# A 12-stage decoder on one core: head maxima subtracted by broadcast weights, a rebuilt last attention stage, new tables, loads and order

## The reference

```
log_D[t, s] = cs[t] - cs[s] + igate[s]    (s <= t)
D = exp(log_D - max_s log_D);   C = (q k^T / 4) * D
h = (C / max(|sum_s C|, exp(-max))) v;  y = per-head layernorm(h) * weight
```

## Time and profile before

| | us |
|---|---|
| median of 3 runs | 1081.8 |
| the profiled execution | 1080.39 |
| its span, first to last instruction | 1078.4 |
| PE busy | 921.6 (85%) |
| PE weight loads busy | 687.3 (64%) |
| DVE busy | 570.5 (53%) |
| ACT busy | 440.2 (41%) |
| POOL busy | 47.4 (4%) |
| mean granted TensorE clock | 0.93 of full speed |

### The profile page before, as it was taken

The page is one execution under the profiler, slowest core; times in us unless marked ns, Lnnn a source line. Parts: engine busy times, 40 slices in busy tenths (PEclk is TensorE's granted clock), DMA queues, the critical chain, the costliest instruction groups (busy, mean ns, idle before and its releaser), DMA issues. The chain is left out here.

```text
span 1078.4 us, 20461 instructions
## 1 busy us (share of the span) xinstructions
PE 921.6 (85%) x8328; PEld 687.3 (64%) x8328; DVE 570.5 (53%) x1589; ACT 440.2 (41%) x897; POOL 47.4 (4%) x68
## 2 busy tenths in 40 slices
PE   6689899899988898988778978988998888898782
PEld 4246578778877584666426745876888766784441
DVE  5744535654356376364554864665425458364347
ACT  2036415354554462361224333533355553632332
POOL 0300000000010000000000000001001000000000
PEclk9699979999999998995969999999999999999875
DMA  9000000301001101121000000030100110000000
GB/s 336 27 2 1 2 2 1 157 2 36 1 18 57 76 1 40 41 88 55 1 1 12 1 2 2 2 156 2 35 2 19 60 73 2 1 1 1 1 1 19
DMA packets 6829, 35.97 MB, mean 33 GB/s; under 512 B 721, under 2 KB 4305, under 8 KB 5458
## 3 DMA queue, kind: packets, MB, share of 16 engines
q1 hardware_dynamic: 6738, 34.68, 8.7%
HBM read 34.15 MB, written 0.52 MB: 32 GB/s over the span
## 5 line engine op out<-in xcount | busy, mean ns | idle before, releaser
L660 PE MATMUL bank<-xT,weights_F 128*128 128x256 f32 x832 | 201.9, 386 | 0.7 <-DVE small L1285 0.7
L660 PEld LDWEIGHTS bank<-xT,weights_F 128*128 128x128 f32 x832 | 152.5, 193 | 23.6 <-issue 4.3
L668 PEld LDWEIGHTS bank<-weights_F,p 128*128 128x128 f32 x1088 | 133.9, 192 | 16.8 <-issue 5.6
L668 PE MATMUL bank<-weights_F,p 128*128 128x128 f32 x1088 | 140.6, 278 | 3.2 <-ACT p L1890 2.3
L1742 ACT ACTIVATE p<-bank 128x512 f32<-128x512 f32 x160 | 84.0, 602 | 115.4 <-PE bank L506 101.4
L1330 DVE SCALAR_TENSOR_TENSOR res<-bank,comb,res 128x128 f32<-128x128 f32 x184 | 55.9, 345 | 74.7 <-PE bank L668 72.5
L1814 ACT ACTIVATE p<-bank 128x512 f32<-128x512 f32 x72 | 42.9, 598 | 99.1 <-PE bank L660 98.6
L1171 DVE TENSOR_REDUCE m_wide<-bank 128x4 f32<-128x512 f32 x96 | 60.3, 683 | 43.1 <-PE bank L767 35.3
L1346 DVE TENSOR_TENSOR p<-p,bank 128x512 f32<-128x512 f32 x72 | 49.3, 685 | 49.1 <-PE bank L660 26.8
L1890 ACT ACTIVATE p<-bank 128x512 f32<-128x512 f32 x64 | 36.5, 598 | 44.6 <-PE bank L660 44.5
L1179 DVE TENSOR_REDUCE mx<-bank 128x4 f32<-128x512 f32 x64 | 39.9, 682 | 27.8 <-PE bank L500 27.6
(11 more groups left out here) (323 smaller groups left out, 1441.5 us busy)
## 6 DMA issues: line engine op xcount, KB each, us to landing
weights_F<-in_L1f SPq DMA_DIRECT2D x2, 4096.0 KB, 13.2
weights_F<-in_L0f SPq DMA_DIRECT2D x2, 3456.0 KB, 13.1
weights_F<-in_L2f SPq DMA_DIRECT2D x2, 3456.0 KB, 11.4
weights_Y<-in_L1x_kv SPq DMA_DIRECT2D x2, 1024.0 KB, 10.3
weights_Z<-in_L1x SPq DMA_DIRECT2D x2, 1024.0 KB, 11.3
weights_Y<-in_L2a SPq DMA_DIRECT2D x2, 898.0 KB, 4.5
weights_Z<-in_L2x SPq DMA_DIRECT2D x2, 449.0 KB, 3.5
weights_L3m<-in_L3m SPq DMA_DIRECT2D x2, 288.0 KB, 6.2
```

The lines of the kernel that those rows point to most:

```text
L660: m = mm(b[:, k * NT:(k + 1) * NT], W[weight][:, f:f + P], s.xT[:], start=True, stop=True)
L668: m = mm(b[:, tk(u)], h[:, tk(u)], w, start=k == 0, stop=k == len(chunks) - 1)
```

## The change

Edits, in the order of the diff. `pick` gets 8 columns, `delta8`, `ones_bf` and `zeros_bf` go. In every softmax `pick_maxima` becomes a plain copy `mT` of the turned maxima, 128 x 128. `less_maxima` becomes 16 products of 128 columns instead of 4 of 512: the weights are one column of `pick` broadcast to 32 x 128, the moving operand is `mT`; banks, and so row groups, alternate within each head. In L1x the scores of a head now come first and the subtraction after them, head by head. The bias rows move into stream b's L0a. L3x: the context's part of the gate logits moves ahead of the turned x, with the two context gates summed once by POOL; `units` subtracts by broadcast weights too, four products in a row for each bank; `retrieved` has values and ones as 128 x 32 weights and the probabilities as moving operand; ACT copies the result to SBUF (`oT`), PE turns it back (`turned_back`), DVE normalises it straight from PSUM. Spreading xT over heads goes from DVE to ACT, four activations of 128 x 256. `use` loads tables for silu and gelu explicitly, ahead of the wait. The memsets of `vz` go from DVE to POOL. xT and L0a's weights are loaded before the constants, ctx_tok last. PE's waits for constants and masks move to where they are used. All of `TURN_ORDER` is new: PE's order now ends `a1 b12`, where it ended `a3 b3 a1 b1`; ACT's ends `a1 b17`, where it ended `a3 b3 a1 b1`.

```diff
...
-        "a2 b4 a1 b1 a3 b2 a1 b1 a1 b2 a1 b2 a1 b1 a1 b4 a13 b3 a1 b1 a5 b12 a4 b3 a4 b2 a9 b4 a1 b5 a2 b2 a1 b2 "
-        "a2 b1 a1 b5 a7 b3 a2 b1 a1 b2 a1 b2 a1 b1 a1 b2 a3 b7 a1 b2 a1 b3 a1 b2 a1 b1 a1 b1 a6 b1 a5 b5 a1 b1 a1 "
...
-                def less_maxima(st, u, banks, blk=0, first=False):
+                def less_maximum(u, i, b, j, last):
+                    return mm(b[:, j * T:j * T + T], const("pick")[rows32(i), j:j + 1].to_broadcast([32, P]), s.mT[rows32(i), u],
+                              start=False, stop=last)
+
+                def less_maxima(st, u, banks, blk=0):
                     pe.wait_ge(*freed(st, "mT", u))
-                    for i, b in enumerate(banks):
-                        m = mm(heads(b[:], 4), const("ones")[rows32(i), 0:T], s.m_diag[rows32(i), u], start=first, stop=not first)
-                        if not first:
-                            filled(m, st, "t", u, blk, i)
+                    for j in range(4):
+                        for i, b in enumerate(banks):
+                            m = less_maximum(u, i, b, j, j == 3)
+                            if j == 3:
+                                filled(m, st, "t", u, blk, i)
...
+                    if pair == 1:
+                        rows = lambda a, e: s.p[0:1].rearrange("p a b -> p (a b)")[:, a:e]
+                        pe.wait_ge(*weights("rows"))
+                        b = opened("act", "rows", 2)
+                        for k in range(2):
...
+                        filled(m, "rows", 2)
+                        yield
+                        filled(mm(opened("dve", "rows", 0)[:], ones_row, rows(0, 512), start=True, stop=True), "rows", 0)
+                        yield
+                        b = opened("dve", "rows", 1)
+                        mm(b[:, 0:384], ones_row, rows(512, 896), start=True, stop=False)
+                        pe.wait_ge(*ready("small"))
+                        pe.wait_ge(*ready("L3a"))
+                        pe.wait_ge(*freed("rows", 2))
+                        mm(b[:, 128:256], s.kT[:, 0:T], W["L2x_o"], start=False, stop=False)
+                        filled(mm(b[:, 256:384], s.kT[:, T:2 * T], W["L3a_o"], start=False, stop=True), "rows", 1)
+                        yield
...
                     def scores_t(u):
                         banks = [opened("act", "L1x", "t", u, 0, n) for n in range(4)]
-                        less_maxima("L1x", u, banks, first=True)
                         for j in range(4):
                             for n, b in enumerate(banks):
                                 r, c = n % 2, 4 * (n // 2) + j
-                                m = mm(b[:, j * T:j * T + T], s.k64[rows64(r), c, tk(u)], s.q64[rows64(r), c, tk(u)],
-                                       start=False, stop=j == 3)
+                                mm(b[:, j * T:j * T + T], s.k64[rows64(r), c, tk(u)], s.q64[rows64(r), c, tk(u)], start=True, stop=False)
+                            if j == 0:
+                                pe.wait_ge(*freed("L1x", "mT", u))
+                            for n, b in enumerate(banks):
+                                m = less_maximum(u, n, b, j, True)
                                 if j == 3:
                                     filled(m, "L1x", "t", u, 0, n)
...
-                    yield from tail("L3a")
+                    yield from tail("L3a", lambda: gate_logits_of("L3x", 1, s.ctxT))
+
+                def gate_logits_of(st, k, src):
+
+                    if k:
+                        if turn == 0:
+                            pe.wait_ge(S("L3x_context_gates"), 1)
+                        pe.wait_ge(*ready(st))
+                    for part in range(2):
+                        b = opened("dve", st, "gates", part) if k else ring.bank((pair, st, "gates", part))
+                        for u in range(NS):
+                            a = 16 * k + 8 * part
+                            m = mm(b[rows32(u), 0:T], W["L3x_gates32"][:, a:a + 32], src[:, tk(u)], start=k == 1, stop=k == 0)
+                        if not k:
+                            filled(m, st, "gates", part)
 
...
-                    pe.wait_ge(*ready("L3x"))
                     pe.wait_ge(*freed("L3a", "xT"))
-                    b = opened("dve", "L3x", "gates")
-                    for part in range(2):
-                        for k in range(3):
-                            for u in range(NS):
-                                a = 16 * k + 8 * part
-                                m = mm(b[rows32(u), part * T:part * T + T], W["L3x_gates32"][:, a:a + 32],
-                                       (s.ctxT if k else s.xT)[:, tk(u)], start=k == 0, stop=k == 2)
-                    filled(m, "L3x", "gates")
-                    yield
-                    yield
+                    gate_logits_of("L3x", 0, s.xT)
                     yield
...
-                            filled(mm(heads(b[:], 4), const("ones")[rows32(u), 0:T], s.m_diag8[rows32(u), 4 * half:4 * half + 4],
-                                      start=False, stop=True), "L3x", "D", i)
+                            for j in range(4):
+                                h = 4 * half + j
+                                m = mm(b[:, j * T:j * T + T], const("pick")[rows32(u), h:h + 1].to_broadcast([32, P]),
+                                       s.gates[rows32(u), 5], start=False, stop=j == 3)
+                            filled(m, "L3x", "D", i)
 
                     def retrieved(u):
-                        b = opened("dve", "L3x", "o", u)
+                        b = opened("act", "L3x", "oT", u)
                         for half in range(2):
                             pe.wait_ge(*freed("L3x", "s", 2 * u + half))
                             for j in range(4):
-                                h = 4 * half + j
-                                m = mm(b[:, 17 * h:17 * h + 17], s.p[:, 2 * u + half, j * T:j * T + T], s.v17[:, u, h],
-                                       start=True, stop=True)
+                                m = mm(b[rows32(j), half * T:half * T + T], s.v_ones[:, u, 4 * half + j],
+                                       s.p[:, 2 * u + half, j * T:j * T + T], start=True, stop=True)
+                        filled(m, "L3x", "oT", u)
...
+                    def turned_back(u):
+                        b = opened("dve", "L3x", "o", u)
+                        pe.wait_ge(*freed("L3x", "oT", u))
+                        for half in range(2):
+                            m = tr(b[:, half * T:half * T + T], s.qk[:, u, half * T:half * T + T], IDENT)
                         filled(m, "L3x", "o", u)
...
+                    turned_back(0)
+                    yield
+                    turned_back(1)
+                    yield
                     yield from tail("L3x")
...
-            pe.wait_ge(*weights("con"))
-            pe.wait_ge(S("masks"), 5)
...
-                    o.count(dve.tensor_tensor(s.m_diag[:, u], among(b[:, 0:T], 4), over(const("pick"), T), ALU.mult),
-                            free(st, "mT", u))
+                    o.count(dve.tensor_copy(s.mT[:, u], b[:, 0:T]), free(st, "mT", u))
...
-                    yield
-                    spread_heads(s.bd_c, s.xT, sem("L3x_bd"), mask16)
...
-                    o.count(dve.scalar_tensor_tensor(s.m_diag8, among(gt[:, 5], 8), -1.0, over(const("delta8")[0:64], T),
-                                                     ALU.mult, ALU.mult), sem("L3x_m_diag"))
-                    for u in range(NS):
-                        o.count(dve.tensor_copy(s.v17[:, u, :, 0:DC], heads(s.ctx_tok[:, u], HC)), sem("L3x_v17") if u else None)
+                    for u in range(NS):
+                        o.count(dve.tensor_copy(s.v_ones[:, u, :, 0:DC], heads(s.ctx_tok[:, u], HC)), sem("L3x_v") if u else None)
...
-                    for i in (0, 3, 1):
+                    for i in (0, 3, 1, 2):
                         unit(i)
                         yield
-                    keep(0)
-                    yield
-                    unit(2)
-                    yield
                     n, m = s.small[:, :, 0:8], s.small[:, :, 8:16]
-                    done = keep(1)
+                    out = [heads(bank("L3x", "o", u)[:, 0:NT], HC) for u in range(NS)]
+                    dve.wait_ge(*freed("L3x", "mx"))
+                    minus = [o.count(dve.scalar_tensor_tensor(n[:, u], out[u][:, :, DC], -1.0, s.small[:, u, 32:40], ALU.mult, ALU.max))
+                             for u in range(NS)]
+                    for u in range(NS):
+                        dve.wait_ge(*minus[u])
+                        done = o.count(dve.tensor_tensor(n[:, u], out[u][:, :, DC], n[:, u], ALU.max))
                     dve.wait_ge(*done)
-                    out = [heads(x[:, 0:HC * 17], HC) for x in held]
-                    for u in range(NS):
-                        o.count(dve.scalar_tensor_tensor(n[:, u], out[u][:, :, DC], -1.0, out[u][:, :, DC], ALU.mult, ALU.max))
```

(47 more changed lines are left out.)

96 lines of the change are left out of this document (34 added, 62 removed), and 54 rows, old and new, of the table TURN_ORDER.

## The result

| | before | after |
|---|---|---|
| median, us (4 runs each) | 1081.92 (1080.71 to 1086.34) | 1035.29 (1025.53 to 1038.56) |
| ratio | | 0.9547 [0.9478, 0.9616] |
| profiled execution, its span | 1080.39, 1078.4 | 1035.02, 1033.0 |
| mean granted clock | 0.93 | 0.94 |

What follows compares the result with a forecast made beforehand. PE was taken to bound the kernel, busy 921.6 of 1078.4 us. Start -2.6, PE's other work +2.5, DVE in softmaxes -3, ACT +2 and end -9 made -10.1: 1080.4 to 1070.3, median forecast 1071, range 1045 to 1092.

Steps and rivals of the forecast that it cites:

- The order elsewhere: New step order outside start and end: taken as 0, the work being the same; bounds -20 and +15 us.
- fifth rival: The new order closes PE's gaps, a fifth of the 100 us idle in the middle: 1050 us; chance 0.15.
- My own sign for it: If PE's idle time in the middle moved by more than 10 us, the order was worth something.
- both count as hidden here: L3x in turn 0: DVE's loss of `m_diag8` (1.2 us a stage) and of the spreading was given no gain.
- The end: -9: Last L3x stages: 48.4 us side by side become 28.5 for b's alone plus 11 for a's; bounds -14 and +1.
- fourth rival: b's last L3x alone takes longer than 38 us, PE's clock staying at half: 1084 us; chance 0.20.
- about 11 us: PE work that a's last L3x adds to the stretch before, beside b's L3a.
- The subtraction: +4.2: Subtraction of maxima in the softmaxes: +0.13 us a call for 32 calls, changes of form at about 0.11 us.
- +4 in L1x: Scores and subtraction alternating by head: 7 more changes of form in each of 8 calls, half their cost taken.
- second and third rivals: On the subtraction: loads bound it (1107, chance 0.05); a load never hides behind its own rows' product (1116, chance 0.02).
- The start, -2.6: First loads and memsets: first matmul 1.6 us earlier, near 5.2, and 1 us for the bias rows' waits.
- ACT, +2: Six more table loads (7.7 us) and 9 us of L3x copies, mostly hidden; +17 with no cover.

Runs made afterwards that it cites:

- a_l1x: The kernel after, with the 16 subtractions of each L1x call put ahead of its 16 scores; 1025.2 us, ratio 0.944.
- a_diag: The kernel after, with the old diagonal operand of 512 columns back in all softmaxes, L3x as changed; 1036.0 us.
- b_sub: The kernel before in its own order, with only the new `pick_maxima` and `less_maxima` in every softmax, L1x too; 1093.8 us, ratio 1.010.
- a_start: The kernel after, with the old first loads, waits and memsets; 1035.7 us.

## Why the prediction was wrong

**The order elsewhere: "I take 0, the work being the same."** This is the step that failed first. On the old code the new order took 33.2 us out of the time up to a's last L3a and 15 to 19 out of the whole. I had its bounds at -20 and +15, and a fifth rival (1050, chance 0.15) in which it closes PE's gaps, but gave it no place in the sum. Even that rival had the smaller half of the mechanism: up to the end of a's first L3x the same work costs 7.9 us less of idle and 19.1 us less of busy PE, at a higher granted clock, which "the work being the same" had ruled out. My own sign for it came true: PE's idle time in the middle moved by 27.5 us.

**L3x: "both count as hidden here."** This is the second. PE's products were priced well: retrieval 1.08 us for two samples at the full clock (for 0.9) and two turns each, the gates, and the subtraction in `units` 1.64 us from start to start for a forecast 2.0.

```profile
974.14 1.08 PE L1058 MATMUL bank<-p,v_ones 128*32 128x128 f32 x32
```

But I counted -4.5 us for the first turn and the removal of `m_diag8` as hidden. In the order it now has, b's first stage is 12 us shorter for the rebuild, and the operand is the largest single part. I had priced an operation by its own length, where the price is the hole it opens and the clock behind the hole.

**The end: -9.** It gave 2.4. The last stage alone came out as forecast: from 54 us to 34 in the stretches, 20 less, for my 48.4 to 28.5 (b's stage took 31.5 us, far from the 38 of the fourth rival). The term that was too small is "about 11 us" for a's L3x beside b's L3a: that stretch grew from 77 us to 95, by 18, some 3 of them products of b's L2x moved into it. a's stage took 35.0 us there, for PE work of 27.84 us in the stretch of 35. On the old code this end would have been dearer still: the new order with the old stage costs 18.4, and the rebuilt stage returns 20.5.

**The subtraction: +4.2, and +4 in L1x.** A call costs +0.03 us and not +0.13. The changes of form cost 0.2 us each and not 0.11, so L1x lost 10 us. With one change of form in either, a_l1x (plain copy, broadcast weights) stands 10.8 us below a_diag (diagonal operand): in this order the new subtraction gives some 10 for the 3 I took, and the to and fro in L1x eats it. That is a difference between two sets of runs, and b_sub, in the old order, showed only a loss. The second and third rivals (1107, 1116) are out. With four row groups a load and a product go in 31 ns an instruction; in `units`, where a bank's eight pairs follow one another in one row group, in 103. The third rival took 285 ns for such a pair, and that price was wrong. The rule that it rested on is that of the Trainium skill (TensorE: Matmul & The Clock Gate, Part 3, The mechanism), by which only loads for another row group run ahead. These two figures fit it, and the 129 ns a pair of the down projection, which I held against it, are no less than 103; but no run shows a load and its product apart.

**The start, -2.6.** The first product came at 4.36 for my 5.2, since L0a's weights landed in 3.1 us; the one behind the fills at 8.33 for my 7.3. The fills ended at 6.20, but the constants, third, landed at 6.38, and ACT's first table load (1.28 us) and the activations that this product needs stand behind them. The median doesn't show a gain (a_start).

**ACT, +2.** 83 table loads, as counted, and 16.5 us more of busy time; no run separates their cost.

**The sum** has a slip of its own: 1070.3 + 1.4 is 1071.7, and I wrote 1071.

## What to carry to other kernels

Ask of an operation that goes not only how long it takes but what waits for it, what stands ahead of it in its engine's queue, and what clock PE has behind the hole it opens: here a DVE instruction of 1.2 us, run four times, cost 13 to 15 us. An edit and an order of work that was planned for it have to be costed together: the new order with the old last stage gave back at the end 18.4 of the 33.2 us it had won, and the edit that was worth most in the new order gained nothing in the old one. The same instructions in another order are not the same PE time: look at the granted clock too. Keep products of one row form together; each change between 64 and 32 rows cost 0.2 us.

## What the hardware did that I had not expected

A change between products of 64 rows and of 32 cost 0.2 us at the full clock. The Trainium skill (TensorEngine Tiling (Array Packing), Key Properties) says that changing the tiling mode drains TensorE; the trace agrees, with 1.08 us a round in after, which has two changes, for a quarter of 3.16, 0.79, which has half a change: 0.29 for one and a half. A weight operand that is one column broadcast over 128 goes in 31 ns, near the 27 of the products with values. And after a hole of 3.43 us PE ran at the lower level of its clock in the 10 us from 965 on (granted 0.55), though it was busy for 7.60 of them.
